# A four-layer graph network kernel: VectorE turns its batch loop round before, not after, its part of the next batch's second aggregate half

## What is computed

```
for each of the 32 graphs:
  layer 0: h = relu(ln(x)); agg = eps*h + adj @ h
           x = x + silu(rmsnorm(agg @ W1 + b1) * w) @ W2 + b2      # 256 -> 1024 -> 256
  layer 1: h = relu(ln(x)) @ W.T + b
           att = sigmoid(h@a1 + (h@a2).T + att_b) * adj * masks, rows scaled to sum 1
           x = x + att @ h
  layer 2: 8-head attention of relu(ln(x)), score bias edge*W_e, masked where adj == 0
           x = x + softmax(q k.T/sqrt(32) + adj*W_e) v @ Wo.T
  layer 3: x = x + D^-1/2 adj D^-1/2 relu(ln(x)) @ W3 + b3
```

## Time and profile before

| | us |
|---|---|
| median of three runs | 3600.38 |
| the profiled execution, whole | 3597.0 |
| its span, first to last instruction | 3595.2 |
| TensorE busy in it | 3476.9 (97%) |
| VectorE busy | 2655.5 (74%) |
| ScalarE busy | 2286.0 (64%) |
| GpSimd busy | 939.5 (26%) |

### The profile page before, as it was taken

How to read it: one execution, slowest core, us unless ns; L and a number is a source line. 1 busy time by engine, 2 the same in 40 slices (tenths; PEclk the granted TensorE clock), 3 DMA queues, 4 the chain that set the end, 5 groups by cost and what they waited for, 6 DMA issues and landing times.

```text
span 3595.2 us, 70344 instructions
## 1 busy us (share of the span) xinstructions
PE 3476.9 (97%) x20108; PEld 2548.7 (71%) x20108; DVE 2655.5 (74%) x6698; ACT 2286.0 (64%) x5062; POOL 939.5 (26%) x2379
## 2 busy tenths in 40 slices
PE   6999999999999999999999999999999999999997
PEld 4777677767777776777677777767777777777774
DVE  6777777777777777777777777777777777777774
ACT  4666666666676666666666766666666667666664
POOL 2222331222221223312222212233122222122320
PEclk8999999999999999999999999999999999999999
DMA  3233223232232332232322323322323223233212
GB/s 102 57 86 92 72 64 93 54 94 74 73 82 62 84 92 73 64 92 54 94 74 72 82 63 84 92 72 64 94 53 94 75 72 82 64 83 92 72 54 65
DMA packets 166941, 275.09 MB, mean 77 GB/s; under 512 B 23908, under 2 KB 59876, under 8 KB 166760
## 3 DMA queue, kind: packets, MB, share of 16 engines
q1 hardware_dynamic: 166760, 273.45, 28.7%
HBM read 122.37 MB, written 16.78 MB: 39 GB/s over the span
## 4 chain that ended last, share of the span: by engine, by line
PE 73%; issue 8%; ACT 7%; DVE 7%; DMA 3%; SPq 2%; POOL 0%; DVEq 0%; ACTq 0%; POOLq 0%
PE turn L1334 9%; PE value L1349 6%; PE score L1376 6%; PE front L1229 6%; PE front L1167 6%; PE front L1137 6%; PE front L1138 5%; PE front L1139 5%; PE score L1325 5%; PE score L1322 4%; DMA qk_stack<-qk 3%; ACT prob L634 2%; DVE prob L984 2%; ACT pT L643 2%; PE front L1194 2%
## 5 line engine op out<-in xcount | busy, mean ns | idle before, releaser
L634 ACT ACTIVATE prob<-prob,small 128x512 f32<-128x512 f32 x1024 | 736.2, 719 | 383.0 <-DVE small L984 379.6
L984 DVE CUSTOM_DVE_ANT_0 prob<-score,adj_sb,drv 128x512 f32<-128x512 f32 x1024 | 758.0, 745 | 89.7 <-PE score L1325 78.0
L1334 PE MATMUL turn<-ident,prob 128*128 128x128 f32 x4096 | 624.3, 275 | 13.0 <-ACT prob L634 7.9
L1325 PE MATMUL score<-qk_stack 128*128 128x512 f32 x1024 | 592.0, 582 | 22.4 <-DMA qk_stack<-qk 22.3
L1334 PEld LDWEIGHTS turn<-ident,prob 128*128 128x128 f32 x4096 | 480.4, 141 | 133.6 <-issue 41.9
L643 ACT ACTIVATE pT<-turn 128x512 f32<-128x512 f32 x768 | 449.9, 586 | 71.8 <-PE turn L1334 42.4
L1322 PE MATMUL score<-unlinked,neg_mask 128*128 128x512 bf16 x1024 | 390.4, 381 | 14.6 <-DVE small L984 12.4
L744 DVE TENSOR_TENSOR s_lo<-front,s_hi 128x512 fp32r<-128x512 f32 x316 | 216.6, 686 | 169.2 <-ACT s_hi L533 169.2
L1137 PE MATMUL front<-w_hi,s_hi 128*128 128x256 f32 x1024 | 300.3, 293 | 0.2 <-DVE w_lo L744 0.2
L1138 PE MATMUL front<-w_lo,s_hi 128*128 128x256 f32 x1024 | 288.5, 282 | 0.0
L1139 PE MATMUL front<-w_hi,s_lo 128*128 128x256 f32 x1024 | 288.1, 281 | 0.0
(11 more groups left out here) (203 smaller groups left out, 7948.6 us busy)
## 6 DMA issues: line engine op xcount, KB each, us to landing
qk_stack<-qk SPq DMA_DIRECT2D x1024, 128.0 KB, 2.4
adjT_f<-in_adjT SPq DMA_DIRECT2D x32, 1024.0 KB, 5.3
adj_sb<-in_adj SPq DMA_DIRECT2D x32, 1024.0 KB, 7.4
prob<-in_adjT SPq DMA_DIRECT2D x32, 1024.0 KB, 5.2
x_new<-in_x SPq DMA_DIRECT2D x32, 512.0 KB, 4.1
out<-x_out SPq DMA_DIRECT2D x32, 512.0 KB, 3.0
pT<-in_W SPq DMA_DIRECT2D x2, 1024.0 KB, 11.3
rmsw_b<-in_rmsw SPq DMA_DIRECT2D x1, 512.0 KB
```

Of the source, the lines that this page charges most:

```text
L634: act.activation(prob[:, i % 8, :], prob[:, i % 8, :], ACT.Exp, bias=nmax[:, h, n:n + 1], scale=-1.0, accum_out=prsum[:, h, n:n + 1]).then ...
L984: dve.tensor_tensor_reduce(out=prob[:, i % 8, :], in0=SB_[i % 2][:, :], in1=adj_sb[:, n, :], scale=neg_w[:, h:h + 1], scalar=3e38, op0=ALU ...
L1325: pe.matmul(SB_[i % 2][:, :], qk_stack[:, h % 4, 0, tile(n)], qk_stack[:, h % 4, 1, :], start=False, stop=True).then_inc(sc_ps, 1)
L1334: last = pe.transpose(TB[k % 2][:, tile(n)], prob[:, (4 * h + n) % 8, tile(j)], ident[:, :])
```

## The change

In VectorE's program alone, the two steps `aggregated(nx, 1)` and `restore_diagonal(nx)` are taken from the end of `phases` into a function of their own, which is called ahead of the pass that follows. The steps come in the same order as before, with the same semaphores. In the loop, they now stand at the head of the body and not at its tail. In the first pass of the loop they belong to the batch that was aggregated ahead of the loop, and behind the loop they are called once more.

```diff
@@ VectorE, end of phases(t, tf, nx)
                 if b:
                     update3(t)
-                if nx is not None:
-                    aggregated(nx, 1)
-                    restore_diagonal(nx)
+
+            def next_aggregate(nx):
+                aggregated(nx, 1)
+                restore_diagonal(nx)
...
             phases(None, 0, 1, {-4: prepare_signs, 3: prepare_w2, 11: prepare_low, 19: prepare_masks, 27: prepare_shared})
+            next_aggregate(1)
             phases(0, 1, 2)
             with dve.Fori(1, B - 2) as t:
+                next_aggregate(t + 1)
                 phases(t, t + 1, t + 2)
+            next_aggregate(B - 1)
             phases(B - 2, B - 1, None)
             phases(B - 1, None, None)
```

## The result

| | median us | span us | ratio to before (95% interval) |
|---|---|---|---|
| kernel before | 3600.29 (3599.36 to 3601.63) | 3595.2 | |
| changed kernel | 3572.39 (3570.81 to 3573.12) | 3569.2 | 0.9924 (0.9914 to 0.9934) |

The change saves 27.9 us, where 20.4 were forecast. The measured 3572.39 us lies 0.6 us under the low end of the range (3573). So the sign came out as forecast, and the turn is hidden in its new place as forecast. The size was outside the range, and the experiments show that a large part of it has a cause that the prediction didn't name.

The account below looks back on a forecast made before the run. TensorE, busy 97% of the span, was taken as the bound, idle at each pass's first score behind VectorE's turn. 28 x 0.73 = 20.5 us less than the 3600.4 median gave 3579.9, said as 3580 us; range 3573 to 3592.

Parts of the forecast that it names:

- the sign: Whole kernel: faster, 3580 us against a median of 3600.4; chance of faster 0.85.
- The turn holds VectorE's queue for 2.8 us, and that is why line 970 is late: VectorE's loop branch: 2.81 us to the next register operation, so line 970 begins 1.50 us after ScalarE's `qk` is done.
- In its new place it hides in the wait for `T_hi`: Behind the last output update: the turn ends 0.5 to 1.0 us before `T_lo` can start, within VectorE's 3.43 us wait.
- Rivals A and B: At the new turn, the code fetch lands behind the output's store: gain lost, 3600 us (0.07), or slower, 3625 us (0.05).
- Of 1.46 us on VectorE, 0.94 reach the first score and 0.73 the end of the pass: Seam with a turn against batch 1 without: lateness at line 970, first score and pass end; 28 x 0.73 = 20.5 us.
- The range: Total time: 3573 to 3592 us, from 3574 less 1 us of spread up to part of a late fetch.
- C: At the first score: more is gained, all of 0.94 us a turn, 3574 us; chance 0.05.
- Register operations cost nothing, `T_lo` and the copy keep their time: VectorE's seam: two more register operations cost nothing, at most 3.9 us; `T_lo` (0.69 us) and copy (0.42 us) keep places.
- The trace agrees for VectorE, not for ScalarE: At the loop's branch: the rule that a taken branch forces a fetch fits VectorE (2.81 us), not ScalarE (0.2 us).

Follow-up runs that it names:

- e2: Kernel before, with two passes in VectorE's loop body, so 13 turns in place of 28: 3585.54 us, ratio 0.9959.
- e4: Kernel before, with a branch hint at the head of VectorE's loop body, seam in its old place: 3573.33 us, ratio 0.9923.
- e6: Kernel before, with the head of VectorE's loop body put at the start of a block of code, no work moved: 3572.22 us, ratio 0.9922.
- e11: Kernel before, with TensorE's code put 60 instructions further on by semaphore operations: 3594.45 us, a single run.
- e9: Kernel before, with the head of VectorE's loop body 64 instructions behind the start of a block of code: 3579.65 us, ratio 0.9942.
- e1: Kernel before, with only the diagonal's copy moved behind VectorE's turn, the subtraction for `T_lo` left ahead of it: 3596.39 us, ratio 0.9991.
- e7: Changed kernel, with TensorE's code put 60 instructions further on by semaphore operations: 3571.01 us, ratio 0.992.
- e8: Kernel before, with 300 more semaphore operations in each pass on GpSimd, which lengthen its loop body: 3909.23 us, ratio 1.0857.

## Why the prediction was wrong

- *The turn holds VectorE's queue for 2.8 us, and that is why line 970 is late:* right. e2 shows it turn by turn, e4 and e6 by taking the fetch away.
- *In its new place it hides in the wait for `T_hi`:* right, with 1.1 us to spare. The changed kernel's passes of 108.87 us are as long as those of e4 and e6, where nothing is fetched at a turn, so nothing of it is left. Rivals A and B, the fetch behind the store, did not come about: the turns have 2.78 to 3.08 us in the changed kernel and 2.78 to 3.06 before.
- *Of 1.46 us on VectorE, 0.94 reach the first score and 0.73 the end of the pass:* this is the step that failed. The term of the sum that was too small is the 0.73 us a turn; it measures 0.98. The 0.73 came from a reference of one pass, and that pass was some 0.25 us long by itself, for TensorE's fetches of code (e11: 108.84 in place of 109.12). The 0.94 hold as a number (0.98 in the mean of the passes), and all of it reaches the end of the pass. But it isn't VectorE's lateness: in e9 line 970 is as late, and only 0.33 us reach the end of the pass. The text said that the last 0.2 us were not followed, and yet the sum was made with 0.73. With 0.98 it gives 27.4 us and 3573.0, 0.6 us over the measured median.
- *The range:* its low end was worked out from C, the case whose size was right, with only 1 us of spread below it, and C had a chance of 0.05. More references without a turn stood in the trace than batch 1. The pass of batch 0 is 109.68 us long, so two passes of one kind, without a turn, differed by 0.56 us, and that was a warning. Batch 30 has no aggregate half at its end, but its first score comes 1.00 us sooner than the mean of the 28 does (11.76 against 12.76 us). I read batch 30 for line 970 alone.
- *Register operations cost nothing, `T_lo` and the copy keep their time:* right. The changed kernel's passes are no longer than those of e4 and e6.
- *The trace agrees for VectorE, not for ScalarE* (on the fetch behind a taken branch)*:* this reading was wrong. The rule of the Trainium skill, "Runtime: NRT & Kernel Launch", instruction fetch mechanics, speaks of a target that isn't held. In e4 and e6 ScalarE turns in its 0.26 us with no packet in q14, so its code is held, and its turn says nothing against the rule.
- What I did not have at all: two thirds of a turn's price are not VectorE's lateness but a packet of code that meets the copies into `qk_stack` (e9). That the new place of the seam moves this packet ahead of the fourth copy was luck.

## What to carry to other kernels

A loop whose body an engine doesn't hold costs a fetch of code at every turn, here 2.5 to 3.1 us of the engine's queue in place of 0.3. Look for the branch and the next register operation in each engine's queue. If the time between them is of the first kind, move the seam under a wait that covers it, put the body's head at the start of a block, or use a hint. Here all three gave the same, and the last two move no work. Then look where the packets of code that are left fall, since in this kernel they cost more than the turn itself.

A pass that lacks the thing you want to price is a good reference only if all else in it is the same. Check its length against a second such pass, and look for DMA issues or copies that take longer than their siblings; in this kernel TensorE's 20 packets of code all come where code runs for the first time, 13 ahead of 318 us and 7 behind 3419 us, and here some fell beside SyncE's issues.

## What the runs showed of the hardware

- A fetch of code is not only a stall of its own engine. Beside one 16 KB packet for TensorE an issue of SyncE's took 0.91 us in one kernel and 1.49 in the other, in place of 0.60. With an 8 KB packet for VectorE inside it, the time from the issue of a 128 KB copy to the first score was 3.12 us in place of 2.41, and less when the packet came sooner in the copy (e1). The runs show the first by shifting TensorE's code (e7, e11) and the second by shifting VectorE's (e9). The sizes are the pages' totals over their packets: 0.33 MB over 20 and 1.32 MB over 161.
- Whether a body of 346 records is held depended on where it starts: held at the start of a block (e6), fetched anew from 64 instructions further on (e9). The Trainium skill, "Runtime: NRT & Kernel Launch", instruction fetch mechanics, says that the held window is two blocks of 256 instructions. By length alone 64 + 346 = 410 instructions would fit into it, and yet e9's turn takes 2.94 us. So the length doesn't tell whether the head is still held at the branch, and the measurement decides. What had taken the head's place no run shows.
- A turn on GpSimd went from 0.27 to 2.5 us when its body grew from 131 to 431 records (e8). In the kernel before, ScalarE with 279 records turns in 0.26 us and TensorE with 755 in 0.27 us, so a length that is dear on one engine isn't on another.
